# Layer pipeline of a two-layer transformer: turning the natural tiles of X ahead of the weighted sums, and writing the rounds out

## What is computed

```python
for i in range(DEPTH):                       # DEPTH = 6
    x = attn_layer(shift_tokens(x), Wqkv[i], q_scale[i], k_scale[i], Wo[i]) + x
    x = ffn_layer(shift_tokens(x), ln_g[i], ln_b[i], W1[i], b1[i], W2[i], b2[i]) + x
...
def attn_layer(x, Wqkv, qs, ksc, Wo):        # 16 heads of 64, windows of 32 tokens
    q = l2norm(q) * qs; k = l2norm(k) * ksc
    q = q * cos * scale + rotate_half(q) * sin * scale
    k = k * cos * inv + rotate_half(k) * sin * inv
    out = local_attention(q, k, v)           # softmax over own and previous window
    return out @ Wo
```

## Time and profile before

| | us |
|---|---|
| median of 3 runs | 2736.19 |
| lowest and highest | 2731.33, 2745.01 |
| the profiled execution, its own time | 2730.72 |
| its span | 2728.9 |
| mean granted TensorE clock | 0.912 of full speed |

### The profile page before, as it was taken

The page is one execution under the profiler, slowest core; times in us unless marked ns, Lnnn a source line. Parts: engine busy times, 40 slices in busy tenths (PEclk is TensorE's granted clock), DMA queues, the critical chain, the costliest instruction groups (busy, mean ns, idle before and its releaser), DMA issues.

```text
span 2728.9 us, 53797 instructions
## 1 busy us (share of the span) xinstructions
PE 2169.6 (80%) x21684; PEld 1154.6 (42%) x21780; DVE 1973.4 (72%) x2087; ACT 1509.5 (55%) x1863; POOL 1492.2 (55%) x1031
## 2 busy tenths in 40 slices
PE   4768875888998989888889889889988756678734
PEld 1111123555555555555555555555555411111334
DVE  1766628888888888888888888888889426676211
ACT  2255564566676666666766676666766321455600
POOL 5500017777776776777776777777777234100033
PEclk7787897999999999999999999999999866897967
DMA  4100000000001000100010000000000001000133
GB/s 149 60 19 25 13 2 1 17 2 17 2 2 26 17 2 2 26 2 17 1 26 2 17 2 9 19 17 2 1 9 2 1 18 67 22 27 13 32 92 86
DMA packets 55828, 59.08 MB, mean 22 GB/s; under 512 B 13142, under 2 KB 45012, under 8 KB 55508
## 3 DMA queue, kind: packets, MB, share of 16 engines
q1 hardware_dynamic: 53444, 50.77, 6.1%
q0 software_dynamic: 2128, 4.72, 0.7%
HBM read 44.07 MB, written 11.01 MB: 20 GB/s over the span
## 4 chain that ended last, share of the span: by engine, by line
PE 36%; POOL 19%; DVE 17%; issue 16%; ACT 9%; DMA 2%; SPq 1%; POOLq 0%; DVEq 0%; ACTq 0%
PE bank L735 5%; PE bank L706 4%; PE bank L859 4%; DVE big L1463 4%; PE bank L923 4%; PE bank L933 4%; POOL big L580 3%; POOL big L597 3%; POOL big L581 3%; DVE big L1569 3%; POOL small L590 2%; ACT big L1180 2%; ACT pxs L1305 2%; PE bank L976 2%; DVE small L1563 2%
## 5 line engine op out<-in xcount | busy, mean ns | idle before, releaser
L1463 DVE TENSOR_REDUCE big<-bank 128x1 f32<-128x512 f32 x512 | 327.7, 685 | 199.3 <-PE bank L706 195.3
L602 POOL TENSOR_TENSOR sc<-sc,small 128x1024 f32<-128x1024 f32 x96 | 263.4, 2744 | 365.4 <-DVE small L1605 365.4
L859 PE MATMUL bank<-wqk,xs 128*128 128x512 f32 x768 | 359.2, 610 | 13.6 <-ACT xs L1261 8.3
L933 PE MATMUL bank<-pxs,mw 128*128 128x256 f32 x1536 | 366.2, 382 | 0.0
L1296 ACT ACTIVATE sc<-sc 128x1024 f32<-128x1024 f32 x96 | 101.5, 1057 | 464.0 <-DVE sc L1595 463.9
L933 PEld LDWEIGHTS bank<-pxs,mw 128*128 128x128 f32 x1536 | 291.1, 192 | 102.7 <-issue 71.9
L1180 ACT ACTIVATE big<-bank 128x1024 f32<-128x1024 f32 x256 | 250.2, 1026 | 140.1 <-PE bank L720 137.1
L1569 DVE TENSOR_TENSOR big<-big,rotCl 128x2048 f32<-128x2048 f32 x96 | 226.2, 2356 | 78.1 <-POOL big L581 78.1
L706 PE MATMUL bank<-pxs 48*128 48x512 bf16 x512 | 183.6, 439 | 117.1 <-DVE big L1463 74.0
L1563 DVE TENSOR_REDUCE small<-big 128x32 f32<-128x2048 f32 x96 | 219.0, 2281 | 39.5 <-ACT big L1274 30.2
L1584 DVE TENSOR_TENSOR big<-big,small 128x1024 f32<-128x1024 f32 x192 | 246.5, 1284 | 1.1 <-POOL small L592 1.1
(11 more groups left out here) (244 smaller groups left out, 3945.1 us busy)
## 6 DMA issues: line engine op xcount, KB each, us to landing
wqk<-in_L_ffn_Wqkv SPq DMA_DIRECT2D x12, 512.0 KB, 4.4
pxs<-part_rows SPq DMA_DIRECT2D x64, 96.0 KB
pxs<-part_rows SPq DMA_DIRECT2D x64, 64.0 KB
wqk<-in_L_ffn_w SPq DMA_DIRECT2D x16, 256.0 KB, 3.0
wvt<-in_wv_layers_t SPq DMA_DIRECT2D x6, 512.0 KB, 4.7
wol<-in_L_ffn_Wo SPq DMA_DIRECT2D x6, 512.0 KB, 5.8
part_rows<-big SPq DMA_DIRECT2D x24, 128.0 KB
part_rows<-sc SPq DMA_DIRECT2D x24, 128.0 KB
```

The lines of the kernel that those rows point to most:

```text
L602: pool.tensor_tensor(p3, p3, rden(i).unsqueeze(2).broadcast_to([P, LH, 64]), ALU.mult).then_inc(l_pn, 1)
L859: m = pe.matmul(bank[:, 2 - 2 * half + c, :], xs[:, b % 2, WIN + i * P:WIN + (i + 1) * P], wqk[:, (2 * half + c) * 512:(2 * half + c + 1) ...
L933: m = pe.matmul(bank[:, 6, part * 2 * P:(part + 1) * 2 * P], mw[:, 2 * (a % 4) + s, a // 4, :], pxs[:, part, a, s, :], start=(a == 0 and s ...
L1463: dve.tensor_reduce(nm[:, qt, 2 * p + r:2 * p + r + 1], bank[:, 4 + r, :], AX.X, ALU.max, negate=True).then_inc(a_mx, 1)
```

## The change

`turn_windows` moves on TensorE from behind `weigh` to right behind `project`, and `windows` on ScalarE from behind `weighed` to right behind the exponent. The waits follow: `turn_windows` waits for `l_e`, `weigh` for the copy of the turned tiles (`l_xe`), and `scores` for the first half of T-2's weighted sums instead of the tiles' copy. Two semaphore steps (`settle`) come in, one in `scores` and one in `turn_windows`. And the loops on the chip over the layers, one on each of five engines, are written out.

```diff
@@ layer_slots
-            with eng.Fori(0, DEPTH - 1) as l:
+            for l in range(DEPTH - 1):
@@ SyncE's loads
-            with sp.Fori(1, DEPTH) as l:
+            for l in range(1, DEPTH):
@@ TensorE
             def scores(T, it, i):
-                if not (isinstance(T, int) and T == 0):
-                    pe.wait_ge(l_xe, T)
+                if not (isinstance(T, int) and T < 2):
+                    pe.wait_ge(l_pc, 2 * T - 3)
+                elif T == 1:
+                    pe.wait_ge(l_xe, 1)
+                settle(pe)
@@
             def turn_windows(T, b, i):
-                if isinstance(T, int) and T == 0:
-                    pe.wait_ge(l_e, 1)
-                else:
-                    pe.wait_ge(l_pc, 2 * T - 1)
+                pe.wait_ge(l_e, T + 1)
+                settle(pe)
@@ TensorE's slot
                         project(it + k // TILES, ...
+                turn_windows(T, b, i)
                 if feeds:
                     feed(fed, fl, i, 2)
                 if mixes:
                     mixing(it, l, b, i, 1)
                 if not (first and i == 0):
                     pe.wait_ge(l_pt, T)
-                    pe.wait_ge(l_e, T + 1)
+                    pe.wait_ge(l_xe, T + 1)
...
                     weigh(T - 1, i + 3)
                 if feeds:
                     feed(fed, fl, i, 3)
-                turn_windows(T, b, i)
@@ ScalarE's slot
                 exponentials(T, i)
+                windows(T, i)
...
                         weighed(T - 1, it if i else it - 1, (i - 1) % TILES, half)
-                windows(T, i)
```

## The result

| | before | changed |
|---|---|---|
| time, median, us | 2733.76 (2729.27 to 2745.01, 4 runs) | 2807.24 (2791.80 to 2812.05, 4 runs) |
| ratio | 1 | 1.0254 [1.0213, 1.0295] |
| span of the profiled execution, us | 2728.9 | 2806.1 |
| mean granted TensorE clock | 0.912 | 0.905 |

The change costs 73 us. The direction was forecast, the size was three times too small (+24 us), and the time lies above the range.

What follows compares the result with a forecast made beforehand. The prediction took a ring of VectorE and GpSimd to set the slot's length. Its terms, -10 + 13 + 10 + 7 + 4 = +24 us on 2736.2, gave 2760 us, range 2722 to 2782 (forecast's own 2748 to 2772).

Steps and rivals of the forecast that it cites:

- The loop, -10: At the 4 jumps back of the layer loop: writing it out saves 2.5 us each, -10 us in all.
- The 0.4 us that I took off: Slot behind a jump: some 0.4 us shorter than its like, cutting the gain per jump from 2.9 to 2.5 us.
- no slot of 20 us is left at the old jumps: Sign to look for at the four old loop jumps: their slots of 20 us would be gone.
- I take the number of them as it is and add nothing: TensorE's stops for code in written-out rounds: their number stays as it is, adding 0 us.
- worse, by code and clock: Rival, chance 0.13: code stops in the long straight program cost up to 29 us, plus TensorE's lower clock; 2785 us.
- Ordinary slots 2, +13 by a lost lock: Slot 2 of 12 ordinary rounds: L1564 comes behind GpSimd's L581, making L1569 1.1 us late; +13 us.
- lock won: Rival, chance 0.22: L1564 is not held behind L581 in ordinary slots 2, the other terms stand; +11, 2747 us.
- are in time at nearly all slots: TensorE's scores seldom hold up VectorE, so removing the idle 1.50 us before L915 buys next to nothing.
- b=3, slot 2, +2.0 each: Slot 2 of 5 rounds with the next layer's tables: TensorE idles until E, then runs at lower clock; +10 us.
- b=0, slot 2, +1.4 each: Slot 2 of 5 fed rounds with weights: `weights` starts 1.4 us later, with keys, queries and scores behind it; +7 us.
- Slot 3, +0.2 each: Slot 3 of 22 rounds: mean_of ends later, putting L306 off to about E+1.45 from E+1.20; +4 us.
- faster, by TensorE's idle time: Rival, chance 0.12: TensorE bounds the stack, so the 53.4 us before L915 come back less new waits; 2715 us.

Runs made afterwards that it cites:

- E1: The kernel before with only the loops over the layers written out, the turned tiles left in place: 2724.40 us, ratio 0.9972.
- E2: The changed kernel with the loops kept on the chip, so only the move: 2776.41 us, ratio 1.0185.
- E6: The kernel before with the move made in slot 3 only, loops on the chip: 2733.62 us, ratio 0.9995.
- E7: The kernel before with the move made in slot 2 only, loops on the chip: 2771.64 us, ratio 1.0140.
- E3: E2's kernel with the transposes put behind mixing on TensorE and their copy behind the raw copies on ScalarE: 2772.23 us, ratio 1.0154.
- E4: The changed kernel with two 512 KB weight loads held until the scores of slot 0 of the fourth round are done: 2784.56 us, ratio 1.0224 of before.

## Why the prediction was wrong in size

**The loop, -10: a failed step.** In the kernel before it is right in sign and place: the slots with the jump are 3.0 us shorter each in E1 (2.9 forecast). The 0.4 us that I took off for the slot behind the jump rest on round 10 alone, where it was 17.84 us; behind the other jumps it was 19.07, 19.08 and 18.82. Alone the loop gave -6. In the changed kernel the gain is not there: one of my signs was that no slot of 20 us is left at the old jumps, and all four are still 20.39 us or longer. What failed is "I take the number of them as it is and add nothing", the price of nothing on TensorE's stops. The rival "worse, by code and clock" was the one whose mechanism came true, with another size. The number of stops does not tell the kernels apart (inside the scores 16 in the changed kernel; with the loop 10 before, 6 in E2, 15 in E6 and E7), but four of them take 3.7 to 5.0 us and lower the clock, and they are no longer hidden. By the rows a stop is hidden as far as its consumer has room: the 11.1 us of stops in E1 and the 19.1 in E6 leave VectorE's slots nearly as they were, and the 34.9 us of the changed kernel are felt. The page "Runtime: NRT & Kernel Launch" of the Trainium skill (Instruction fetch mechanics) calls the crossing of a block of code mostly hidden; if these stops are such crossings, TensorE's rows do not agree in any kernel here. What hides them in E1 is the room of the scores.

**Ordinary slots 2, +13 by a lost lock: a failed step.** The small operation won in 10 of 11 slots, in round 6 by 0.08 us, and the term is nearly 0. The mechanism exists and has its price (E3: +1.0 us in each such slot, 1.1 forecast), but the forecast put its chance too high: `mixing` ended no earlier than worked out, `residual` started at E+4.90, as forecast, but from there to the small operation it took 2.92 us, not the 3.04 of the earlier trace rows: E+7.82, where I had 7.88 to 7.97, against L581 at E+7.90. A question of 0.1 us is not one to give a chance of 2 in 3 to. In both kernels the small operation ends 0.04 to 0.05 us behind the end of L580 (1196.25 against 1196.21 before, 916.68 against 916.63 now): it gets its turn at the border of L580 and L581, if it is there by then. The rival "lock won" was right in this, and its 2747 was too low by 60 us, because it shared the error above and the next one.

**The error behind it: the path over `weigh` was not followed.** The prediction says of the scores that they "are in time at nearly all slots" and leaves it there. In b=0 I followed `weigh`, the copies, keys, queries, scores; in the ordinary slots I stopped at `residual` and the lock. Followed to the end it was readable before: the scores of round 6 ended 1.8 us ahead of need, and the new order makes `weigh` as much later (E+6.80 against E+5.02), since the wait for E and the transposes stand ahead of `ffn_out` and `mixing` too. The slot then has next to nothing over. By itself that cost nothing in the ordinary slots: in E2 eight of the ten slots 2 of b=1 and b=2 are 16.34 to 16.57 us long, as before, and the two of 17.92 are those in which `ffn_out` took 4.44 us behind an idle time of 2.3 us (granted clock 0.58 from 1199 to 1203). With the stops of the changed kernel it cost +1.7 us in b=2 and +4.0 in b=1.

**b=3, slot 2, +2.0 each.** Right in size, +1.94 in E2 and +2.06 in the changed kernel, and in part by luck: 2.0 was the middle between two bounds. `ffn_out` ran at half speed, as the upper bound had it, and `mixing` did not (2.09 us instead of 1.89); and up to 1 us of the loss is VectorE's wait for the scores, which the forecast did not have. TensorE, round 11, answering to the earlier trace rows:

```profile
1291.52 0.66 PE L916 MATMUL bank<-ident,xs 128*128 128x128 f32 x2 [6.10 <-DVE sc L1596]
1291.97 5.32 PE L977 MATMUL bank<-hT,w 128*128 128x512 f32 x6
```

**b=0, slot 2, +1.4 each.** Mis-sized: +4.2 in E2, +3.3 in the changed kernel. In four of the five rounds the slot is 19.9 us long, as in round 8, where TensorE reads:

```profile
1068.28 1.65 PE L946 MATMUL bank<-wol,wvt 64*128 64x128 f32 x16 [2.20 <-ACT pxs L1306]
1069.85 1.97 PE L870 MATMUL bank<-ident,big 128*128 128x128 f32 x8
```

`weights` starts at E+9.00, where it started at E+7.03 before (round 4): 2.0 us later, and not 1.4. Behind the idle 2.20 us it takes 1.65 us and the keys 1.97; in four of five rounds before it was 1.16 and 1.09 (the 1.63 of the earlier trace rows is the fifth). TensorE in round 12, the longest:

```profile
1365.60 0.53 PE L916 MATMUL bank<-ident,xs 128*128 128x128 f32 x2 [2.30 <-DVE sc L1596]
1365.93 4.36 PE L977 MATMUL bank<-hT,w 128*128 128x512 f32 x6
...
1376.14 2.08 PE L946 MATMUL bank<-wol,wvt 64*128 64x128 f32 x16 [2.20 <-ACT pxs L1306]
```

Here the idle 2.30 us ahead of `ffn_out` are followed by 4.36 us instead of 2.74 as well, and `weights` takes 2.08. VectorE ends up waiting 4.03 us for these scores. I took 1.4, the shift that I had worked out, of 0.5 to 2.5, and left the lower clock to the range's upper end, though the idle time that I worked out for TensorE there (2 us) was nearly that ahead of b=3's slow matmuls (2.60).

**Slot 3, +0.2 each.** Mis-sized: +0.6 to +0.8 in E2. L306 starts at E+2.16 in the changed kernel (round 6: 928.73 against 926.57) instead of E+1.20; the projection ends 0.97 us behind E, and that comes from slot 2 (it ends 0.84 us behind E in E7, where nothing was moved in slot 3); the two transposes add only the rest. As in the slots 2, I took slot 3 with its beginning unchanged.

**The sum.** Terms as E2 shows them for a layer: 4.2 + 0.4 + 0.3 + 1.9 in slots 2 and 0.8 + 0.6 in the slots 3 of b=2 and b=3, where the forecast had 1.4 + 1.1 + 1.1 + 2.0 and 0.2 each; less 0.7 and 1.0 in the slots 3 of b=0 and b=1. The forecast had +34 for the move alone. E2 came to +46, and its profiled execution, which these terms are of, to +34: there the forecast's sum agrees while its terms do not, which is luck. It is the other 34 us, of the two halves together, that put the time outside the range.

What those are can be read from the rows of the profiled executions. VectorE waits 3.15, 4.65, 3.85 and 5.13 us for the scores in slot 2 of rounds 5, 9, 13 and 17, 16.8 us in all, where E2 has 0.5. It waits 3.65, 3.27, 3.64 and 3.23 us for L298 right behind them, and 2.72 and 2.62 in rounds 10 and 14, with projections of 5.3 to 6.4 us instead of 3.70 ahead; in the other rounds up to 21 it is at most 1.02, so the lower clock behind the stops makes up some 13 us. The short stops in slot 2 of b=2 add 7. And writing the jump out gives less in the new order: in E2 the four slots with a jump are 18.95 us long, against 17.99 in round 21 without one, so the jump costs 1.0 us there and not 3.2, which is 9 us less to gain. Together that is close to the 42 us of the table, less what b=0 gives back. Only the stops beside the loads were put to a test (E4). Why the clock falls behind some stops and not behind others stays open.

The rival *faster, by TensorE's idle time* is out: 53.4 us of TensorE's waiting were removed and not one came back. "Where is the engine that ends the slot" beat "which engine has the largest share".

## What to carry to other kernels

Follow a delayed instruction to the last of its consumers and compare the delay with the room there: a term that stops at the first neighbour misses the path that runs out of room second. Room that looks idle also pays for stops that nobody scheduled, so two edits that are each measured alone can cost much more together. And a short VectorE operation beside a long GpSimd one belongs clearly before or clearly behind it, with something long that runs beside it in between.

## What the runs showed of the hardware

- In written-out rounds TensorE stops inside runs of small matmuls for 0.5 to 2.2 us, at a fixed count of instructions: in each layer at the same places, one matmul earlier each time (x43, x42, x41, x40, x39 in E4's section). The rounds of a loop have such stops too (10 of up to 1.9 us before). With 1 MB of weight loads issued 2.3 and 2.7 us before it begins (round 9) the same stop takes 3.7 to 5.0 us in four rounds; with the loads held, 1.7 to 2.0. Behind the four long ones TensorE's next eight matmuls took 5.95 to 6.38 us instead of 3.70, at a granted clock of 0.62 in round 9.
- A VectorE operation of 128x32 takes 0.14 to 0.18 us in the rows above, and 1.88 us when it comes 0.52 us behind the start of a GpSimd operation of 2.35 us; 0.08 us ahead of it, it takes 0.18. The transpose of 128x1024 that began 0.07 us behind L581 (916.65 against 916.58) and lay wholly beside it took its usual 1.25 us. The page "SBUF - State Buffer" of the Trainium skill (SBUF: two separate sides) has GpSimd and those VectorE operations that run in a 2-port mode or have two inputs in SBUF exclude each other at a shared port pair, whoever starts first; the small operations agree with it, and the transpose, which has one input, was not held.
- After 6.1 us of idling, TensorE's six matmuls of `ffn_out` took 5.32 us where they take 2.74; after 2.30 us in round 12 they took 4.36, and after 2.30 us in round 8 and 2.29 in round 6 2.74. So the length of the idle time alone does not tell. The granted clock in the first case was at the lower of its two levels, 1.2 of 2.4 GHz (TensorE's windows view: us, busy, clock, DMA):

```profile
1291.50:1294.50 3.00, 2.98 (x5) 0.50 0.00 0
```
